# Where the row scales of the first experts are computed, and which engine applies them

## The reference, cut to what matters

```
def activation_quant(x):
    scale = 127.0 / jnp.maximum(jnp.max(jnp.abs(x), axis=-1, keepdims=True), EPS)
    return jnp.clip(jnp.round(x * scale), -128.0, 127.0) / scale

def expert_ffn(x, gw, uw, dw):
    gate = bitlinear(x, gw)
    up = bitlinear(x, uw)
    activated = up * jnp.square(jax.nn.relu(gate))
    return bitlinear(activated, dw)
```

## Time and profile before

| | |
|---|---|
| median of 3 runs | 451.5 us (450.04 to 451.88) |
| the profiled execution, its own time | 454.02 us |
| its span | 452.2 us |
| granted TensorE clock, mean | 0.943 |
| busy: TensorE, VectorE, ScalarE, GpSimd | 82%, 74%, 47%, 31% of the span |

### The profile page before, as it was taken

One profiled execution on the slowest core, in us unless ns is written; L12 is line 12 of the kernel. 1 busy time (PEld: TensorE's weight loads), 2 busy tenths in 40 slices (PEclk: granted clock), 3 DMA queues, 4 the chain that ended last, 5 costly groups with the idle time before them and its releaser, 6 DMA issues.

```text
span 452.2 us, 10550 instructions
## 1 busy us (share of the span) xinstructions
PE 373.0 (82%) x3676; PEld 257.6 (57%) x3677; DVE 335.7 (74%) x836; ACT 213.0 (47%) x467; POOL 139.3 (31%) x149
## 2 busy tenths in 40 slices
PE   2497888833777778997999999999999989729995
PEld 1376666731344445774466475575664778516784
DVE  6849999888889889579776886887777525672453
ACT  1689999461577788684021131132122221324441
POOL 1110000023477774311092440431421410143334
PEclk9999999855699999999999999999999999957999
DMA  8995680402146551271022022021120201333011
GB/s 259 404 407 196 235 321 5 188 1 64 37 157 223 181 161 48 77 250 40 0 94 94 1 95 92 4 94 43 53 94 10 87 1 48 140 95 92 25 37 37
DMA packets 17183, 50.77 MB, mean 112 GB/s; under 512 B 2104, under 2 KB 6464, under 8 KB 15088
## 3 DMA queue, kind: packets, MB, share of 16 engines
q1 hardware_dynamic: 14272, 42.46, 26.3%
q0 software_dynamic: 2864, 7.68, 5.9%
HBM read 43.44 MB, written 6.69 MB: 111 GB/s over the span
## 4 chain that ended last, share of the span: by engine, by line
PE 56%; ACT 11%; DVE 10%; issue 8%; DMA 7%; POOL 5%; SPq 2%; DVEq 0%; ACTq 0%; POOLq 0%
PE bank L960 16%; PE bank L1174 8%; PE bank L976 6%; PE bank L1048 5%; DMA raw<-in_L_ffn_w_dram 3%; ACT W L1207 3%; PE bank L987 3%; PE bank L1001 2%; POOL y_rows L591 2%; PE bank L819 2%; PE bank L1027 2%; PE bank L1011 2%; ACT pnat L1193 2%; PE bank L830 1%; POOL xg L584 1%
## 5 line engine op out<-in xcount | busy, mean ns | idle before, releaser
L1714 DVE TENSOR_TENSOR roped<-bank,cst 128x512 f32<-128x512 f32 x96 | 61.1, 684 | 29.0 <-PE bank L960 28.0
L612 POOL TENSOR_TENSOR WE<-WE,wT 128x512 f32<-128x512 f32 x32 | 42.6, 1359 | 81.6 <-DMA WE<-_L_ffn_expert_masks_dram 81.6
L960 PE MATMUL bank<-XNT_hi,AW_hi 128*128 128x512 f32 x96 | 41.8, 435 | 0.5 <-DVE XNT_lo L1766 0.5
L1343 ACT ACTIVATE qrT<-bank 128x512 f32<-128x512 f32 x16 | 8.7, 596 | 62.2 <-PE bank L987 62.2
L960 PE MATMUL bank<-XNT_lo,AW_hi 128*128 128x512 f32 x96 | 37.8, 393 | 0.0
L960 PE MATMUL bank<-XNT_hi,AW_lo 128*128 128x512 f32 x96 | 37.5, 391 | 0.0
L976 PE MATMUL bank<-roped,MW 128*64 128x512 f32 x128 | 31.0, 605 | 0.0
L1337 ACT ACTIVATE prob<-prob 128x512 f32<-128x512 f32 x16 | 10.1, 632 | 44.3 <-DVE prob L1724 44.3
L1048 PE MATMUL bank<-VW,ctxT 128*128 128x256 f32 x128 | 30.7, 385 | 0.0
L584 POOL DMA_INDIRECT xg<-x_rows,owner_b x23 | 22.7, 985 | 23.5 <-DMA x_rows<-xrow 14.3
L960 PEld LDWEIGHTS bank<-XNT_hi,AW_hi 128*128 128x128 f32 x96 | 18.0, 187 | 19.9 <-issue 11.4
(11 more groups left out here) (305 smaller groups left out, 880.2 us busy)
## 6 DMA issues: line engine op xcount, KB each, us to landing
raw<-in_L_ffn_w_dram SPq DMA_DIRECT2D x8, 1536.0 KB, 8.9
fold<-in_L_xattn_fold_dram SPq DMA_DIRECT2D x8, 1024.0 KB, 5.0
WE<-_L_ffn_expert_masks_dram SPq DMA_DIRECT2D x8, 1024.0 KB, 5.3
kv<-in_keys_values_dram SPq DMA_DIRECT2D x8, 656.0 KB, 7.7
yg<-y_rows SPq DMA_DIRECT2D x8, 256.0 KB, 4.8
x_tok<-pay SPq DMA_DIRECT2D x8, 256.0 KB, 2.2
X<-in_x_dram SPq DMA_DIRECT2D x4, 256.0 KB, 11.8
x_rows<-xrow SPq DMA_DIRECT2D x1, 516.0 KB, 4.9
```

The costliest lines, as they stand in the source:

```text
L612: pool.tensor_tensor(WE[:, e], WE[:, e], wT[:], ALU.mult).then_inc(WE_ready, 1)
L960: mm = pe.matmul(bank[g][:], a[:, k, c * P:(c + 1) * P], b[:, k, g * 512:(g + 1) * 512], start=k == 0 and i == 0, stop=k == 1 and i == 2)
L1714: ins = dve.tensor_tensor(roped[n][:, r, :].rearrange("p (b s) -> p b s", s=S), src, cst[:, None, at:at + S].to_broadcast([P, 8, S]), ALU. ...
```

## The change

GpSimd no longer scales any block; ScalarE scales all 23. In ScalarE's order the scaling of block j+1 stands ahead of the relu of block j+3, in every turn; the scaling of block 0 stands after the first relus and rows. On VectorE the small steps of a block no longer follow its row maximum. L1672 of block j-1 stands between the two large products of block j, the other three small steps of block j-1 stand between the second product of block j and its row maximum. TensorE's `turn_hidden` waits for ScalarE's signal for each block.

```diff
@@ gpsimd @@
             for j in range(NBLK + 8):
-                b = j - 7
-                if 0 <= b < NBLK and b % 2 == 0:
-                    pool.wait_ge(h_scale_ready, b + 1)
-                    pool.tensor_scalar(hid[b % 4][:], hid[b % 4][:], hs[b % 4][:, 4:5], MAGIC, ALU.mult, ALU.add).then_inc(hid_scaled, 1)
@@ tensor: turn_hidden @@
-                if r % 2:
-                    pe.wait_ge(hid_acted, n + 1)
-                else:
-                    pe.wait_ge(hid_scaled, n + 1)
+                pe.wait_ge(hid_acted, n + 1)
...
-                    turn_hidden(r, 2 * i + r // 2)
+                    turn_hidden(r, j)
@@ scalar @@
+            scale_hidden(0)
             for j in range(NBLK):
                 hidden_rows(j, j % 2)
                 if j >= NBLK - 2:
                     high_part(0, j - NBLK + 2)
                 if j + 4 < NBLK:
                     rows(j + 4, j % 2, j % 4)
+                if j + 1 < NBLK:
+                    scale_hidden(j + 1)
                 if j + 3 < NBLK:
                     relus(j + 3, (j + 3) % 2)
-                if j % 2 == 0 and j + 1 < NBLK:
-                    scale_hidden(j + 1)
                 outputs(j)
@@ vector @@
+            def row_scale(r):
+                h = hs[r]
+                link.after(link.n - 1)
+                return link.note(dve.tensor_scalar(h[:, 2:3], h[:, 1:2], h[:, 0:1], EPS, ALU.mult, ALU.max))
+
+            def its_inverse(j, r, scale):
+                h = hs[r]
+                link.after(scale)
+                inverse = link.note(dve.reciprocal(h[:, 3:4], h[:, 2:3]))
+                dve.tensor_scalar(h[:, 5:6], h[:, 2:3], block_w[:, 1, bass.ds(j, 1)], None, ALU.mult)
+                link.after(inverse)
+                dve.tensor_scalar(h[:, 4:5], h[:, 3:4], h[:, 0:1], QMAX, ALU.mult, ALU.mult).then_inc(h_scale_ready, 1)
...
                 dve.wait_ge(relu_ready, j + 1)
-                link(dve.scalar_tensor_tensor(hid[r][:], bank[2 - par][:], 0.0, relu[par][:], ALU.max, ALU.mult))
+                gated = link.note(dve.scalar_tensor_tensor(hid[r][:], bank[2 - par][:], 0.0, relu[par][:], ALU.max, ALU.mult))
+                if not first:
+                    scale = row_scale((r + 3) % 4)
+                link.after(gated)
                 dve.tensor_tensor(hid[r][:], hid[r][:], bank[4 - par][:], ALU.mult).then_inc(hid_done, 1)
+                if not first:
+                    its_inverse(j - 1, (r + 3) % 4, scale)
                 dve.wait_ge(hid_done, j + 3)
-                link(dve.tensor_reduce(h[:, 1:2], hid[r][:], AX.X, ALU.max, apply_absolute_value=True))
-                link(dve.tensor_scalar(h[:, 2:3], h[:, 1:2], h[:, 0:1], EPS, ALU.mult, ALU.max))
-                inverse = dve.reciprocal(h[:, 3:4], h[:, 2:3])
-                dve.tensor_scalar(h[:, 5:6], h[:, 2:3], block_w[:, 1, bass.ds(j, 1)], None, ALU.mult)
-                link(inverse)
-                dve.tensor_scalar(h[:, 4:5], h[:, 3:4], h[:, 0:1], QMAX, ALU.mult, ALU.mult).then_inc(h_scale_ready, 1)
+                link.note(dve.tensor_reduce(hs[r][:, 1:2], hid[r][:], AX.X, ALU.max, apply_absolute_value=True))
...
+            link.after(link.n)
+            its_inverse(NBLK - 1, (NBLK - 1) % 4, link.note(dve.tensor_scalar(...)))
```

More of the change, by code:

```diff
@@ L898, in _ @@
                 j = 4 * ROUNDS + k
-                turn_hidden(j % 4, j // 2)
+                turn_hidden(j % 4, j)
                 if j + 4 < NBLK:
@@ L1659, in _ @@
             link(dve.tensor_tensor(gate[:, 1, :], gate[:, 1, :], gate[:, 0, :], ALU.mult))
+            def row_scale(r):
[9 more added lines that the diff above has]
+                dve.tensor_scalar(h[:, 4:5], h[:, 3:4], h[:, 0:1], QMAX, ALU.mult, ALU.mult).then_inc(h_scale_ready, 1)
             def hidden(j, r):
-                par, h = r % 2, hs[r]
+                par = r % 2
+                first = isinstance(j, int) and j == 0
                 if not isinstance(j, int) or j >= 4:
@@ L1686, in _ @@
                 hidden(j, j % 4)
+            link.after(link.n)
+            its_inverse(NBLK - 1, (NBLK - 1) % 4, link.note(dve.tensor_scalar(hs[(NBLK - 1) % 4][:, 2:3], hs[(NBLK - 1) % 4][:, 1:2],
+                                                                              hs[(NBLK - 1) % 4][:, 0:1], EPS, ALU.mult, ALU.max)))
             dve.sem_inc(roped_ready, 2)
```

## The result

The changed kernel takes 457.13 us (median of 4 runs, 456.01 to 458.25), the kernel before 451.13 us (4 runs, 450.04 to 451.88). The ratio is 1.0139, 95% interval 1.0102 to 1.0176: slower by 1.4%, 6.0 us. The forecast was 456.8 us and +5.3.

What follows compares the result with a forecast made beforehand. GpSimd and VectorE were taken to share the bound at 2.95 us a block; the change closes a ring of 3.16. 19 x 0.21 = 4.0, +1.7 start, -0.4 end, +5.3 on 451.5 gives 456.8 us, range 453.0 to 461.5.

Steps and rivals of the forecast that it cites:

- The bound of before: Blocks between relu 3 and relu 22 before the change: GpSimd and VectorE share the bound, at 2.95 us a block.
- The ring: Relu n+1 waits for scaling n-1, whose factor needs relu n: 3.16 us a block, bounds 3.00 to 3.43; chance 0.63.
- From relu to product: Ring's first term, from relu n's start to VectorE's first product: 0.70 us.
- The scaling from idle: Ring's last term, ScalarE's scaling on an idle engine until the relu behind it starts: 0.63 us, bounds 0.54 and 0.70.
- the signs that were announced: Changed profile: relus every 3.1 to 3.2 us, some 0.8 us idle before ScalarE's scaling and VectorE's first product, GpSimd waiting for y.
- The start: Relu 0 to 3: block 0's scaling on ScalarE makes its turning 1.6 us late and relu 3 1.7 us late.
- The end: Relu 22 to the last y: 7.9 us in place of 8.25, counted as -0.4 us.
- The total: At the last scatter: 4.0 from the pace, +1.7 start, -0.4 end, +5.3 us; 456.8 us, 1.2% slower.
- The fullest engine: Rival for the pace: it falls to ScalarE's 2.69 us a block, giving 447.9 us, faster; chance 0.07.
- The ring with its upper terms: Rival for the pace: small steps do not fit the gaps, 3.43 us a block, 461.9 us; chance 0.12.
- TensorE's clock: Rival at the start: clock rises later after 1.6 us idle, two blocks at half clock, 459.2 us; chance 0.08.
- The rule that was weighed: VectorE's next instruction waits until the pipeline is empty; ring's third term would be 1.20 and a block 3.29 us.

Runs made afterwards that it cites:

- VectorE's half alone: Kernel before with only VectorE's part of the changed kernel, the new placing of the small steps; 450.54 us, ratio to before 0.9991.
- the other half alone: Changed kernel with VectorE's code as before: ScalarE scales all blocks ahead of the relu; 450.56 us, ratio to before 0.9978.
- the opened ring: Changed kernel with two ScalarE calls exchanged, relu j+3 ahead of the scaling of block j+1; 455.43 us, ratio to before 1.0074.
- the early scaling: Changed kernel with block 0's scaling moved ahead of the relu of block 2; 455.24 us, ratio to before 1.0101.
- the two fastest kernels: Changed kernel with block 0 scaled early and either all small steps between the two products (447.75 us) or VectorE's code of before (447.90 us).
- the shortened ring: Changed kernel with all four small steps of block j-1 between block j's two products, 449.85 us; with block 0 scaled early too, 447.75 us.
- the work behind: Changed kernel with one unused row maximum more for each block on VectorE, directly behind the block's own; 456.91 us, ratio to before 1.0132.

## Why the prediction was right, point by point

*The bound of before.* GpSimd and VectorE were said to share it. VectorE's half alone, with VectorE lighter, kept 2.95 us, so VectorE was not what held the pace; the other half alone, with VectorE as it was, gained 0.13 us a block once GpSimd had no scalings. So this step of the prediction was wrong for VectorE: GpSimd and the odd blocks' path through relu and scaling were the bound of before. No run separates those two, but the relus of the kernel before show both: nine of the ten turns that hold an odd block's scaling take 3.07 or 3.08 us, the turn of the opened ring above, and the nine turns between them 2.35 to 3.45, 2.83 in the mean. The forecast did not rest on this.

*The ring.* 3.16 us was predicted and 3.14 measured, as the mean of 19. The sum came out that well because terms were off in opposite ways. From relu to product was taken at 0.70 us and is 152.37 - 151.76 = 0.61 in nine turns and 0.68 in ten. The scaling from idle was estimated at 0.63 and takes 154.86 - 154.14 = 0.72. It has the same length, 0.81 us, with and without idle time ahead of it, so the 0.70 from the row of the same instruction was the better guide than the nearest other one. The first to the second product took the 0.73 that was forecast, with the small step inside it. From there to the factor it was 153.89 + 0.21 - 153.10 = 1.00 for the 1.07 forecast, all of it because L1664 to L1667 took 0.19 for the 0.26 of the earlier trace rows, and 0.04 for 0.03 to ScalarE. Of the signs that were announced, VectorE's idle time ahead of its first product came, 0.77 or 0.84 us in a turn, and GpSimd's waits ahead of the scatters for y grew from 13.3 to 28.3 us. ScalarE's wait for the factor came too, but with 0.4 to 0.5 us in most turns and not with the 0.8 announced. The prediction's own figures gave that: ScalarE's six instructions take 2.69 us, which leaves 0.41 of a turn of 3.10.

*The start.* +1.7 us was predicted, +2.25 measured. The mechanism was right, and the early scaling took most of it back. The turning of block 0 started 7.68 us after relu 0, for 7.63 forecast. What the sum had too small stands behind it. The turning was put at 0.9 us, half at the low clock, and from its start to hidT it took 1.15, all at the low clock (granted clock 0.50 from 117.0 to 120.4). The scaling took 0.71 for 0.65. And relu 3 waited another 0.17 us for the gate and up matmuls of block 3, which stand behind the late turning, took 1.91 us from 118.51 at the low clock, for 1.03 at the high one, and ended at 120.42. The sum had let relu 3 wait for ScalarE's instructions alone.

*The end.* -0.4 us was predicted, 0.0 measured. The scaling of block 22 started 4.97 us after relu 22, for 5.0 forecast. Its turning then started 0.29 us behind the end of the scaling, with weight products in front of it on TensorE, so that hidT of block 22 was through 7.29 us after relu 22, for 7.1 forecast. The down matmuls and the last y took another 0.93 us, for 0.8.

*The total.* +5.3 us predicted, +5.8 in the stage and +6.0 by the medians. Nothing behind the stage absorbed it. The pace gave 0.4 us less than forecast, the start 0.55 and the end 0.4 more. That the forecast of 456.8 us lies 0.3 from the measured 457.13 is in part luck, as it started from 451.5 us, and the kernel before measured 451.13 beside the changed one.

*The rivals.* The fullest engine did not set the pace: the change took VectorE from 90% to 75% of the stretch and made the kernel slower. The Trainium skill, page "Perfetto Trace Analysis", section "Identifying the Most-Contended Engine", would have us relieve the engine of highest occupancy; with VectorE that gained nothing in any run here. Occupancy did not name the limit in the two fastest kernels either: ScalarE is the fullest engine in both, at 96% and 95%, but the pace is that of the shortened ring in one and of VectorE, 93% busy, in the other. The ring with its upper terms did not come, since the small steps do fit into the gaps. TensorE's clock rose late, but less late than this rival needed. Counted from relu 0 the low clock lasted longer than before: block 3's gate and up matmuls took 1.29 us in the kernel before, where the granted clock was 0.78 from 120.90 to 122.24, and 1.91 in the changed one. From 121.7 us on, 1.2 us after relu 3, it was 1.00, so the low clock cost only within the start term.

*The rule that was weighed.* By the Trainium skill, page "VectorE: DVE Perf Modes", section "The DRAIN you can't avoid", the step behind the second product would start no earlier without a wait than with one. The trace has it 0.60 us behind (153.70 - 153.10) against 0.73 for an instruction that waits for the one in front. The measurement decides: the ring came to 3.14 and not 3.29. The prediction did not weigh the whole section, which also says that a next instruction that is not held starts earlier; with that sentence the trace agrees.

*What stays open.* TensorE's granted clock is 0.94 in the 28 us behind the experts in the changed kernel's profile and 1.00 in that of before. The time from the last y to the end is 267.0 us there against 265.7, but it ranges from 264.8 to 266.9 over the other profiles without a relation to the change. The lower clock there is no mark of the change: it is 0.94 in five other profiles of this study, too, VectorE's half alone among them, whose time is that of before, and 1.00 with the work behind, which is as slow as the changed kernel. Whether any of the 6 us comes from there was not tried.

## What to carry to other kernels

When work is moved later on one engine and earlier on another, write down for each wait which turn of the loop its producer belongs to, and close the circle: here one place of delay on VectorE and one place forward on ScalarE turned a slack of two blocks into a ring of 3.1 us, while each move alone was free. Occupancy does not show this; the idle time ahead of the instructions and who ends it does. A busy share below 100% does not clear an engine either: VectorE set the pace at 93%, because its instructions that wait for each other leave 0.03 to 0.04 us between them. And filling such gaps with small steps can pay only where the engine's own sequence sets the pace, and only down to the next limit. Before that, the result that others wait for should come out as early as it can, even if the engine then needs longer for a block.

## What the runs showed of the hardware

- Small steps of VectorE behind a large instruction that they don't wait for start 0.60 to 0.61 us behind it in the changed kernel, and the product behind them is not late for them: 0.73 us from product to product with the small step inside (152.37 to 153.10), as without it in the earlier trace rows. From the inverse to the factor of the activations it is 0.19 or 0.20 us in all turns of the changed kernel; in the kernel before it is 0.26 or 0.27 in 16 blocks, as in the earlier trace rows, and 0.19 or 0.20 in the other seven. Why is not shown.
- ScalarE's scaling took 0.81 us in all 23 places, between 0.809 and 0.815, behind a wait or behind another instruction.
- The beginning of the stage moved by up to 4 us between profiled executions whose code up to there is the same, more than half of the effect studied here. Intervals within the stage agreed far better: relu 0 to relu 3 took 10.74 or 10.75 us in five kernels that differ up to there only in VectorE's instructions.
